# The D-skip of a Mamba-2 block: VectorE products with a spread row in place of diagonal matmuls, and a new table of fill steps

## What is computed

```python
x = x + weights @ (layernorm(x) @ W + B)       # weights: 4096x4096 from adj: exp(-(1/r - 1)**2 / 0.5) where adj < 1, else 0
xn = layernorm(x)
z, xBC, dt = split(xn @ W_in)                  # 512, 512+2*64, 8
xBC = silu(conv4(xBC)); xh, B, C = split(xBC)  # xh: 8 heads of 64
dt = softplus(dt + dt_bias); A = -exp(A_log)
Y_diag = (C @ B.T * decay) @ (xh * dt)         # within a chunk of the sequence
Y_off  = (C @ state) * exp(A_cum)              # what earlier chunks left in the state
Y = (Y_diag + Y_off + xh * D) * silu(z)        # xh * D is the skip: one D per head
Y = Y * rsqrt(mean(Y*Y) + eps) * norm_w
x = x + Y @ W_out @ W_lin + b_lin
```

## Time and profile before

| | before |
|---|---|
| median of three runs | 2346.95 us |
| the profiled execution | 2347.56 us |
| its span | 2345.8 us |
| TensorE matmul (PE) busy | 2193.8 us, 94% |
| VectorE (DVE) busy | 1819.0 us, 78% |
| ScalarE (ACT) busy | 1564.1 us, 67% |
| GpSimd (POOL) busy | 1146.0 us, 49% |
| product steps L714, two records each | 512 |
| diagonal products L846, two records each | 128 |

### The profile page before, as it was taken

One profiled execution on the slowest core, in us unless ns is written; L12 is line 12 of the kernel. 1 busy time (PEld: TensorE's weight loads), 2 busy tenths in 40 slices (PEclk: granted clock), 3 DMA queues, 4 the chain that ended last, 5 costly groups with the idle time before them and its releaser, 6 DMA issues.

```text
span 2345.8 us, 26329 instructions
## 1 busy us (share of the span) xinstructions
PE 2193.8 (94%) x8940; PEld 1398.6 (60%) x8940; DVE 1819.0 (78%) x2089; ACT 1564.1 (67%) x2545; POOL 1146.0 (49%) x928
## 2 busy tenths in 40 slices
PE   7999999999999999989999999998999997779998
PEld 4544545555555556556766666676766664436786
DVE  5676778787777865324999998999989898897665
ACT  5577686777686845426676867667676867775444
POOL 2101212222231213213988888888988888890000
PEclk9999999999999999999999999999999999899999
DMA  6243233333232323233323232332333221312121
GB/s 236 72 139 99 92 124 100 122 96 125 89 126 89 120 88 135 90 101 111 130 93 126 91 122 86 116 109 94 123 104 114 99 81 37 117 54 99 36 81 45
DMA packets 117496, 241.22 MB, mean 103 GB/s; under 512 B 8771, under 2 KB 66371, under 8 KB 116979
## 3 DMA queue, kind: packets, MB, share of 16 engines
q1 hardware_dynamic: 108290, 207.14, 26.7%
q0 software_dynamic: 8528, 31.36, 3.9%
q10 hardware_dynamic: 544, 1.05, 0.1%
HBM read 219.20 MB, written 20.32 MB: 102 GB/s over the span
## 4 chain that ended last, share of the span: by engine, by line
PE 66%; POOL 10%; DVE 9%; ACT 9%; issue 5%; DMA 1%; ACTq 0%; SPq 0%; DVEq 0%; POOLq 0%
PE ps L714 15%; PE ps L756 10%; POOL dB L2394 6%; PE ps L1000 5%; DVE h L1550 3%; PE ps L878 2%; PE ps L852 2%; POOL acc L2376 2%; PE ps L984 2%; PE ps L738 2%; ACT ps L1738 2%; POOL du L2390 1%; PE ps L782 1%; PE ps L784 1%; PE ps L697 1%
## 5 line engine op out<-in xcount | busy, mean ns | idle before, releaser
L1550 DVE TENSOR_TENSOR_SCAN h<-ps,hst,dB 128x512 f32<-128x512 f32 x512 | 637.5, 1272 | 58.8 <-ACT ps L1738 50.2
L2394 POOL TENSOR_TENSOR dB<-du,bc 128x512 f32<-128x512 f32 x512 | 647.8, 1285 | 61.5 <-DVE h L1550 59.0
L714 PE MATMUL ps<-wgt,msg 128*128 128x512 f32 x1024 | 486.8, 597 | 2.3 <-DVE wgt L1216 2.3
L1738 ACT ACTIVATE ps<-dt,cols 128x512 f32<-128x512 f32 x512 | 351.9, 692 | 179.9 <-DVE h L1550 177.6
L756 PE MATMUL ps<-raw,msg 128*128 128x256 f32 x1792 | 436.4, 379 | 0.9 <-ACT hb L1738 0.9
L1000 PEld LDWEIGHTS ps<-consts,h 128*128 128x128 f32 x2048 | 251.3, 144 | 224.9 <-DVE acc L1512 73.4
L1000 PE MATMUL ps<-consts,h 128*128 128x128 f32 x2048 | 318.5, 281 | 70.7 <-DVE acc L1512 38.0
L756 PEld LDWEIGHTS ps<-raw,msg 128*128 128x128 f32 x1792 | 324.0, 190 | 74.1 <-issue 42.1
L714 PEld LDWEIGHTS ps<-wgt,msg 128*128 128x128 f32 x1024 | 189.7, 191 | 205.7 <-issue 201.8
L1738 ACT ACTIVATE wgt<-wgt 128x1024 f32<-128x1024 f32 x256 | 257.7, 1047 | 52.0 <-DVE wgt L1209 50.8
L2376 POOL TENSOR_TENSOR acc<-acc,part 128x512 f32<-128x512 f32 x174 | 226.3, 1301 | 59.4 <-ACT part L1738 57.9
(11 more groups left out here) (332 smaller groups left out, 3609.8 us busy)
## 6 DMA issues: line engine op xcount, KB each, us to landing
raw<-in_adjT SPq DMA_DIRECT2D x256, 512.0 KB, 3.5
bc<-tmp_bc SPq DMA_DIRECT2D x64, 512.0 KB, 4.8
E<-tmp_bc POOLq DMA_DIRECT2D x32, 512.0 KB, 4.4
xb<-in_xT POOLq DMA_DIRECT2D x8, 512.0 KB, 4.2
tmp_x<-xb POOLq DMA_DIRECT2D x8, 512.0 KB, 3.5
x<-tmp_x SPq DMA_DIRECT2D x8, 512.0 KB, 5.7
tmp_x<-x SPq DMA_DIRECT2D x8, 512.0 KB, 4.9
msg<-in_W SPq DMA_DIRECT2D x4, 1024.0 KB, 10.0
```

Source lines behind the costliest of these rows:

```text
L714: x = e.matmul(f[d].ps[:, :], msg[:, j, d * 128:(d + 1) * 128], wgt[g % NW][:, l, :], start=j == 0, stop=j == NJ - 1)
L1550: e.tensor_tensor_scan(hr[n % 3][:, m, :], PS[4 + k % 2].t[:, :], dBr[k % 4][:, :], hst[:, n % 16, m:m + 1], ALU.mult, ALU.add).then_inc(S ...
L1738: return e.activation(out, in_, func, bias=bias, scale=scale)
L2394: e.tensor_tensor(dBr[k % 4][:, :], du[:, m, :], bcr[i % 3][:, n % 2, :], ALU.mult).then_inc(S("dB"), 1)
```

## The change

It does four things.

1. TensorE's four diagonal products of each chunk (L846) are gone. The first of the eight head products starts the bank instead of adding to it.
2. VectorE makes the skip: per chunk `skip` = X times `Drow` ahead of `xdt`, and `skip` += `tmp` behind the new state; then `tmp` = `skip` + Y stands where `tmp` + Y stood. Two `skip` buffers take turns.
3. `Drow` is D of each column's head, the same in all partitions. It is made once, at the start: the diagonal matrix lies in the memory of `skip0`, one matmul with a matrix of ones (512 columns) spreads it, and VectorE copies it. It takes one more use of `ring_b`. To make room, B has a tile of its own (in memory that `skip1` later takes) and `rows` is loaded by two DMAs in place of one.
4. `FILLS` has ten pairs in place of eight, and the block 0 has a list of its own. Of 64 steps of a block 21 stand at given places now, where 17 did.

A semaphore of a later stage (`b2a`) is merged into another (`b2c`).

```diff
@@ buffers
-        rows = sb(cA, "rows", [128, NROW])
-        Bbc, dtb, Abc = rows[:, 0:256], rows[:, 256:288], rows[:, 288:296]
-        diagD = sb(cA, "diagD", [128, 4, 128])
+        rows = sb(cA, "rows", [128, NROW - D])
+        dtb, Abc = rows[:, 0:32], rows[:, 32:40]
+        Drow = sb(cA, "Drow", [128, 512])
...
+        skip0 = sb(cA, "skip0", [128, 512])
+        cM = ExitStack()
+        Bbc = sb(cM, "Bbc", [128, D])
+        cM.close()
+        skips = [skip0, sb(cA, "skip1", [128, 512])]
+        diagD = skip0[:, :].rearrange("p (m c) -> p m c", m=4)
@@ order
-        FILLS, SEND, ... = ((5, 3), (7, 2), (8, 3), (25, 2), (30, 2), (38, 2), (50, 2), (57, 1)), 58, ...
+        FILLS, SEND, ... = ((1, 1), (5, 2), (7, 2), (8, 3), (25, 2), (30, 2), (32, 2), (38, 4), (50, 3), (57, 2)), 58, ...
...
-            fill = [ssd_at[i] - 1e-6 for i, n in FILLS for _ in range(n)]
+            early = FILLS if ib else ((5, 3), (7, 2), (8, 2)) + FILLS[4:]
+            fill = [ssd_at[i] - 1e-6 for i, n in early for _ in range(n)]
@@ TensorE, ssd: outer
-                    w.wait_ge(S("setup"), 5)
                     w.wait_ge(Y.evac, Y.n - 1)
-                    for m in range(4):
-                        e.matmul(Y.ps[:, m * 128:(m + 1) * 128], cc[:, m, ts_], diagD[:, m, :], start=m == 0, stop=False,
-                                 skip_group_check=True)
                     yield
                     w.wait_ge(S("M"), 4 * ib + s + 1)
                     w.wait_ge(X.evac, X.n)
                     for h in range(8):
-                        i = e.matmul(Y.ps[:, h * 64:(h + 1) * 64], Es[:, h, :], xd[:, h * 64:(h + 1) * 64], start=False,
-                                     stop=h == 7, skip_group_check=True)
+                        i = e.matmul(Y.ps[:, h * 64:(h + 1) * 64], Es[:, h, :], xd[:, h * 64:(h + 1) * 64], start=True,
+                                     stop=True)
@@ TensorE, start
+                    b = drow_use()
+                    w.wait_ge(S("setup"), 5)
+                    w.wait_ge(b.evac, b.n - 1)
+                    e.matmul(b.ps[:, :], one, skip0[:, :], start=True, stop=True).then_inc(b.full, 1)
@@ VectorE, ssd: inner
                     w.wait_ge(S("xdec"), c - 1)
+                    if c < 2:
+                        w.wait_ge(drow_use().evac, drow_use().n)
+                    e.tensor_tensor(skips[s % 2][:, :], X.ps[:, :], Drow[:, :], ALU.mult)
                     e.tensor_tensor(heads(xd[:, :]), heads(X.ps[:, :]), dt[...], ALU.mult).then_inc(X.evac, 1)
@@ VectorE, ssd: outer
                     e.tensor_tensor(h0[0:64, :], hd[:, :], St.ps[0:64, :], ALU.add).then_inc(St.evac, 1)
+                    w.wait_ge(Yo.evac, Yo.n)
+                    e.tensor_tensor(skips[s % 2][:, :], skips[s % 2][:, :], tmp[:, :], ALU.add).then_inc(S("skip"), 1)
                     yield from (None, None)
                     w.wait_ge(Y.full, Y.n)
-                    w.wait_ge(Yo.evac, Yo.n)
-                    e.tensor_tensor(tmp[:, :], tmp[:, :], Y.ps[:, :], ALU.add).then_inc(Y.evac, 1)
+                    w.wait_ge(S("skip"), c + 1)
+                    e.tensor_tensor(tmp[:, :], skips[s % 2][:, :], Y.ps[:, :], ALU.add).then_inc(Y.evac, 1)
@@ VectorE, start
+                    b = drow_use()
+                    w.wait_ge(b.full, b.n)
+                    e.tensor_copy(Drow[:, :], b.ps[:, :]).then_inc(b.evac, 1)
@@ GpSimd, start
-            e.dma_start(rows[:, :], t["rows"].broadcast_to([128, NROW])).then_inc(S("d_rows"), 16)
+            e.dma_start(rows[:, :], t["rows"][:, D:NROW].broadcast_to([128, NROW - D])).then_inc(S("d_rows"), 16)
+            e.dma_start(Bbc[:, :], t["rows"][:, 0:D].broadcast_to([128, D])).then_inc(S("d_rows"), 16)
```

More of the change, by code:

```diff
@@ L271, in build @@
         lane_b = (ccs[0][:, 2:4, :], ccs[0][:, 4:6, :], xdecs[1][:, :])
-        ring_a, ring_b = Ring(PS[2:5], 6 * NB // 2), Ring(PS[5:8], 6 * NB // 2 + 4)
+        ring_a, ring_b = Ring(PS[2:5], 6 * NB // 2), Ring(PS[5:8], 6 * NB // 2 + 5)
         prod = [Ring(PS[0:1], 3 * NB), Ring(PS[1:2], NB)]
@@ L285, in message_use @@
             if ib % 2:
-                return ring_b.use(ib // 2 * 6 + (4 if ib > 1 else 0) + i)
+                return ring_b.use(ib // 2 * 6 + (5 if ib > 1 else 0) + i)
             return ring_a.use(ib // 2 * 6 + i)
@@ L290, in combined_use, with drow_use @@
             return ring_b.use(6 + m)
+        def drow_use():
+            return ring_b.use(10)
         def pre_use(ib, i):
@@ L380, in build @@
         order_first += ["p"] * 8 + ["evac"] + ["pre"] * (NPA - 54)
-        FILLS, SEND, WFIRST, WLAST, EVAC, PREND = ((5, 3), (7, 2), (8, 3), (25, 2), (30, 2), (38, 2), (50, 2), (57, 1)), 58, 0.04, 0.925, 0.97, 0.95
+        FILLS, SEND, WFIRST, WLAST, EVAC, PREND = ((1, 1), (5, 2), (7, 2), (8, 3), (25, 2), (30, 2), (32, 2), (38, 4), (50, 3), (57, 2)), 58, 0.04, 0.925, 0.97, 0.95
         order_a = []
@@ L452, in build @@
         over_a = [(made_by(1, NB).full, made_by(1, NB).n), (ssd_use(NB - 1, 27).evac, ssd_use(NB - 1, 27).n), (ssd_use(NB - 1, 31).evac, ssd_use(NB - 1, 31).n),
-                  (S("hd"), 4 * NB), (S("M"), 4 * NB), (S("xdec"), 4 * NB), (S("halo"), NB + 1),
+                  (S("hd"), 4 * NB), (S("M"), 4 * NB), (S("skip"), 4 * NB), (S("xdec"), 4 * NB), (S("halo"), NB + 1),
                   *((S(f"d_x2_{b}"), 16 * len(range(b, NB, 3))) for b in range(3)), (S("d_m2"), 16 * (NB - 2))]
@@ L1150, in mean_of_bias @@
                 b = end_use(2)
-                w.wait_ge(S("b2c"), 1)
+                w.wait_ge(S("b2c"), 2)
                 w.wait_ge(b.evac, b.n - 1)
@@ L1197, in messages @@
                 yield
-                w.wait_ge(S("d_rows"), 16)
+                w.wait_ge(S("d_rows"), 32)
                 for s in range(4):
@@ L1201, in messages @@
                     w.wait_ge(b.full, b.n)
-                    e.tensor_tensor(msg[:, 4 * ib + s, :], b.ps[:, 0:256], Bbc, ALU.add).then_inc(b.evac, 1)
+                    e.tensor_tensor(msg[:, 4 * ib + s, :], b.ps[:, 0:256], Bbc[:, :], ALU.add).then_inc(b.evac, 1)
                     yield
@@ L1653, in second_matrices @@
                 w.wait_ge(b_tw.evac, b_tw.n)
-                e.tensor_scalar(b2[:, 0, :], b2[:, 0, :], tw[:, 0:1], None, ALU.mult).then_inc(S("b2a"), 1)
-                w.wait_ge(S("b2a"), 1)
+                e.tensor_scalar(b2[:, 0, :], b2[:, 0, :], tw[:, 0:1], None, ALU.mult).then_inc(S("b2c"), 1)
+                w.wait_ge(S("b2c"), 1)
                 e.scalar_tensor_tensor(b2c[:, :], b2[:, 1, :], tw[:, 1:2], b2[:, 0, :], ALU.mult, ALU.add).then_inc(S("b2c"), 1)
```

## The result

The changed kernel takes 2360.09 us (median of 4 runs, 2358.68 to 2361.29) against 2346.7 of the kernel before: ratio 1.0058, interval 1.0045 to 1.0071. So it is slower by 13.4 us, 0.6%. The forecast was 2355.

The account below looks back on a forecast made before the run. ScalarE and VectorE bound each middle block up to the copy of z, TensorE the rest; 0.9 − 2.0 + 11.4 − 1.5 − 0.5 = +8.3 us on the former kernel gave a forecast of 2355, range 2340 to 2373.

Parts of the forecast that it names:

- A: Middle block from second variance to second x tile, set by ScalarE and VectorE: 45.03 us before, 46.23 forecast.
- rival 2: TensorE alone is the bound, so all diagonals and waits are gained: 2315 us; chance 0.15 with its partial form.
- VectorE's additions: New VectorE product and sum per chunk, 0.60 us each; two on the way to z's copy add 1.20 a block.
- The wait: TensorE idles ahead of the second x tile for ScalarE's copy of z, about 4.0 us in one piece.
- The clock: Falls to half speed at the second x tile in each of five middle blocks, costing 2.0 us a block.
- rival 1: The wait comes but the clock holds at 2.4 GHz: 2345.3 us in all; chance 0.25.
- B: Middle block from second x tile to the next block's second variance, set by TensorE: 65.99 us before, 65.07 forecast.
- The middle blocks: Blocks 1 to 5, each 0.28 us longer plus 2.0 for the clock: +11.4 us.
- The start: One more TensorE product of 512 columns, VectorE's copy fitting in beside it: +0.9 us.
- Block 0: Three diagonals go where TensorE works, and the wait for `wgt` comes later: −2.0 us (−5 to +1).
- Blocks 6 and 7: Diagonals partly gained, VectorE's additions on the way: −1.5 us in block 6, −0.5 in block 7.
- so half of the diagonals is lost: Block 6: z's copy ends only 0.5 us ahead of the second x tile, so half the diagonals bring nothing.

Follow-up runs that it names:

- e2: The kernel before with the new fill table alone, diagonals kept: 2346.0 us, ratio 0.9998.
- e5: The kernel before with its diagonals taken out and nothing in their place, so the skip is missing from the result: 2340.2 us, ratio 0.9976.
- e4: The changed kernel with five product steps put directly ahead of the second x tile in blocks 1 to 5: 2341.5 us, ratio 0.9977.
- e6: The changed kernel with 128 matmuls of the diagonals' size and places put back, results overwritten: 2363.6 us, ratio 1.0070.
- e11: Half of the change: VectorE's skip for chunks 1 and 3 only, old table with two steps ahead of the second x tile, new list in block 0: 2343.6 us.
- e3: The changed kernel with 20 useless matmuls ahead of the second x tile in blocks 1 to 5, filling TensorE's wait: 2352.4 us, ratio 1.0031.
- e9: The kernel before with the new fill list in block 0 alone: 2343.0 us, ratio 0.9987.
- e10: e4 with a sixth step ahead of the second x tile and the old table in blocks 6 and 7: 2342.5 us, ratio 0.9981.
- e8: e4 with the sum of skip and state part made by GpSimd instead of VectorE: 2353.5 us, ratio 1.0029.
- e1: The changed kernel with the fill table of before, in block 0 too: 2360.9 us, ratio 1.0059.

## Why the prediction was right, and where it was not

**What bounds the kernel: right.** Two pieces with different owners. A without any skip work on VectorE was 45.03, 45.04 and 45.09 us (before, e2, e5), whatever TensorE had to do in it; with two additions on the way 46.2 to 46.3 (changed kernel, e4, e6); with one, 45.6 (e11). The 99% of TensorE in a block were no proof that it alone was the bound: rival 2 would have shown 107 us a block in e5, and e5 took 109.3 in four of five.

**VectorE's additions: right.** 0.60 us each, two on the way: A was forecast at 46.23 and is 46.31.

**The wait: right, size a little low.** 4.0 us in one piece forecast, 4.58 measured in the first three of the blocks. In the last two it is 2.88, since the clock falls in A as well, and that makes TensorE arrive later.

**The clock: right.** 2.0 us a block taken; by e3 it is 1.9 in the mean of five (1.5 to 2.5). This decided between the forecast and rival 1, and e3 shows it: B is 64.9 us there with the wait filled and all else in it the same. The rule of the Trainium skill on waits between bursts of matmuls (TensorE: Matmul & The Clock Gate, on HAM oscillation) fits the changed kernel: at this wait the clock fell in each of the five blocks. The length of the wait, by which the prediction told forecast and rival 1 apart, is a weaker sign than it took it for. A wait of 2.03 us, behind which the clock had held, was followed by a fall in e9 and in e10.

**The middle blocks: right.** +11.4 forecast, +10.3 measured. B without the fall is 64.9 us, where 65.07 was forecast.

**The start: too low.** +0.9 forecast, 2.0 at the first block's variance, and 1.2 to 2.3 in all kernels with this start. Where the rest beyond the matmul's 0.9 comes from stays open. TensorE's wait for GpSimd's sq at 45.54 grew from 0.32 to 1.43 us, but it doesn't explain the delay: it is 0.32 in e6, with the new start, and 1.26 in e5, with the old one.

**Block 0: right sign, by luck.** I took −2.0 for three diagonals. The diagonals gave 0.7 there (e5). The gain came from the list of block 0, 4.8 us by itself in e2 and 6.7 in e9, which I had not priced at all: I counted steps per piece in the middle blocks, and block 0 has its own list, which I read for the diagonals only. In the changed kernel block 0 gave 4.1 us: the wait of 2.33 us for `wgt` is gone, and 3.6 us less ran at half speed, worth 1.8. The start and block 0 together came to −2.1 against −1.1 forecast.

**Blocks 6 and 7: wrong.** −2.0 forecast, +1.8 measured. Two things failed. The clock was left out of these blocks, and it fell there twice. With the same instructions and without the fall in block 6, e3 takes 151.7 us instead of 153.8 (152.0 before), so 2.0 of the miss are the clock. Whether it falls ahead of block 6's first variance differs between kernels with the same lists there: it did in e4 and e8 too, and not in e6. The other 1.7 are in the term "so half of the diagonals is lost", which was too kind: without that fall the two blocks gained 0.3 and not 2.0. The new table takes 0.7 of it (e2). VectorE's additions take the rest, as far as the waits of TensorE tell: over the two blocks, before and then changed, they are

```profile
PE ps L836 <- DVE hs L1334: 1.6, 1, 1.6
...
PE ps L846 <- DVE hs L1347: 3.0, 3, 1.8
PE ps L677 <- DVE sq L1270: 1.9, 1, 1.9
PE ps L858 <- DVE xdt L1327: 0.7, 1, 0.7
PE ps L748 <- DVE xdt L1327: 0.7, 1, 0.7
```

with more waiting for the new state and for `xdt`, behind `skip` on VectorE. No run takes that apart. The 1.5 us that the kernel without a skip gains here (e5) are no measure of the diagonals either, since the clock fell three times in its blocks 6 and 7 and never in those of before.

**The sum.** The profiled span is 3.2 us longer than the sum had it: 3.8 from blocks 6 and 7 and 1.5 from behind the stage, less 1.1 for the middle blocks and 1.0 for the start and block 0.

## What to carry to other kernels

- An engine that is busy for 99% of a block may be tied with a chain through two others. Before moving work off it, cut the block at the places where another engine releases it, and sum each piece by its owner. The quickest test is the kernel with the work left out (e5): it gives the most that a replacement can bring as long as the order of the rest stays.
- Work taken from an engine in a piece that it doesn't own turns into a wait. In this kernel the clock fell in it or at its end in all five blocks, and the next piece started at half speed. Filling it with useful work from the piece behind turned +13.4 us into −4.3 here (e4).
- A table of fill steps and a swap of work are two changes. Run each alone: here the table's gain of 4.8 us in block 0 hid its loss in the middle and part of the loss by the swap.
- Two runs of one stretch of code can differ by a fall of the clock. Compare the granted clock stage by stage before a difference is put down to the edit: 2.0 of the 7.7 us between e3 and the changed kernel came from a stretch that the edit doesn't touch, and half of what e9 gained in block 0 went in two falls in block 7.

## What the runs showed that was not expected

The clock also fell within piece A, 24 to 27 us behind the second variance, in some blocks, with no wait of TensorE of over 1.1 us ahead of it in that piece. It did so only in kernels with the new table in the middle blocks (the changed one, e2, e3, e4, e6, e8, e10), and in none with the old (before, e1, e5, e9, e11). In e2, where TensorE had slack in A, the block kept its 111.76 us; in e3, where it had none, it was 1.4 to 2.0 us longer. The length of a fall varied as well: most lasted 3 to 4 us, and the first two at the x tile of the changed kernel about 7. In e1 one of about 7 us (0.50 from 711 to 717) lay wholly in B, and that block took 113.8 us instead of 112.2:

```profile
708.54:711.54 3.00, 1.69 (x4) 0.91 0.00 0
711.54:714.54 3.00, 3.00 (x14) 0.50 0.00 0
714.54:717.54 3.00, 3.00 (x9) 0.50 0.02 5
717.54:720.54 3.00, 3.00 (x14) 0.96 0.30 78
```

Why it falls within A stays open; no run took that apart. Nor is there a sharp length of wait behind which it falls: it did in or behind each of three waits of 4.6 us, behind six of eight of 2.7 to 2.9 (e1, the changed kernel and e6), behind one of five of 1.7 (e5), and behind none of 1.5, 1.15 and 1.0 us (e2, e4, e6). At other places it fell behind a wait of 1.90 us in the changed kernel and held behind the same one in e3, and behind one of 2.03 us it held before and fell in e9 and e10.
